# Four layers' tail taken batch by batch: staggered norms, a shorter mix, other places for the activation tables

## What is computed (the reference, cut)

```
x = x + tanh(g_xattn[i]) * xattn_i(layernorm(x), ctx)
x = x + tanh(g_ffn[i])   * ffn_i(layernorm(x))

layer 0: 16-head attention; then six local-attention blocks with feed-forwards
layer 1: a = attend(x -> ctx); c = attend(ctx -> x)
         gate = sigmoid([a, c] @ Wg.T + bg);  result = gate * a + (1 - gate) * c
         ffn: entmax1.5 router over 16 experts (sort, sums, a square root), then gelu
layer 2: attention, then layernorm(result + residual) * gamma + beta
         ffn: top-2 of 8 experts plus a shared one, silu
layer 3: 16-head attention, then top-2 of 8 linear experts
```

## Time and profile before

| | us |
|---|---|
| median of 3 runs | 1364.03 (1363.24 to 1368.13) |
| the profiled execution, its own time | 1366.49 |
| its span in the profile | 1364.5 |
| PE busy | 1259.0 (92%) |
| DVE busy | 973.8 (71%) |
| ACT busy | 933.8 (68%) |

### The profile page before, as it was taken

One profiled execution on the slowest core, in us unless ns is written; L12 is line 12 of the kernel. 1 busy time (PEld: TensorE's weight loads), 2 busy tenths in 40 slices (PEclk: granted clock), 3 DMA queues, 4 the chain that ended last, 5 costly groups with the idle time before them and its releaser, 6 DMA issues. The chain is left out here.

```text
span 1364.5 us, 45293 instructions
## 1 busy us (share of the span) xinstructions
PE 1259.0 (92%) x18140; PEld 906.7 (66%) x18140; DVE 973.8 (71%) x2477; ACT 933.8 (68%) x2301; POOL 744.8 (55%) x753
## 2 busy tenths in 40 slices
PE   6999978999999999999999999999988888999877
PEld 4777635676776777667776776667667767775544
DVE  3666647888888888888888888888843544554766
ACT  5777745677777777777777777777745655643981
POOL 3444437878777877787778877778740042000000
PEclk9999989999999999999999999999999989999998
DMA  4000032222225222522252224222302000000000
GB/s 199 1 2 1 1 109 69 68 63 58 63 61 142 61 63 61 140 60 59 64 143 59 62 62 140 58 61 62 100 9 105 2 1 10 14 0 1 1 1 16
DMA packets 68320, 76.97 MB, mean 56 GB/s; under 512 B 14864, under 2 KB 62992, under 8 KB 67600
## 3 DMA queue, kind: packets, MB, share of 16 engines
q1 hardware_dynamic: 68112, 74.07, 20.4%
HBM read 26.31 MB, written 0.52 MB: 20 GB/s over the span
## 5 line engine op out<-in xcount | busy, mean ns | idle before, releaser
L1073 POOL TENSOR_TENSOR arena<-arena,small 128x512 f32<-128x512 f32 x96 | 100.2, 1044 | 151.1 <-DVE small L956 151.1
L821 ACT ACTIVATE arena<-banks 128x512 f32<-128x512 f32 x96 | 57.4, 598 | 143.8 <-PE banks L653 143.7
L932 DVE TENSOR_TENSOR arena<-banks,rotary 128x512 f32<-128x512 f32 x192 | 131.6, 685 | 31.8 <-ACT arena L791 18.3
L1048 POOL TENSOR_TENSOR arena<-arena 128x512 f32<-128x512 f32 x96 | 122.8, 1279 | 35.9 <-DVE arena L934 35.9
L702 PE MATMUL banks<-arena 64*64 64x32 f32 x6144 | 113.0, 221 | 17.3 <-issue 8.7
L1053 POOL TENSOR_TENSOR arena<-arena 128x512 f32<-128x512 f32 x96 | 122.7, 1279 | 2.2 <-DVE arena L934 2.2
L702 PEld LDWEIGHTS banks<-arena 64*64 64x64 f32 x6144 | 100.7, 135 | 29.4 <-ACT arena L843 12.8
L503 POOL TENSOR_TENSOR arena<-arena,small 128x512 f32<-128x512 f32 x64 | 66.5, 1040 | 86.9 <-DVE small L437 86.9
L616 PE MATMUL banks<-slot,z 128*128 128x512 f32 x192 | 100.9, 607 | 6.9 <-DVE z L1022 3.4
L717 PE MATMUL banks<-arena,slot 128*128 128x128 f32 x768 | 104.0, 278 | 0.5 <-ACT arena L851 0.3
L1060 POOL TENSOR_TENSOR arena<-arena,small 128x512 f32<-128x512 f32 x96 | 100.7, 1049 | 1.2 <-ACT small L831 1.2
(11 more groups left out here) (315 smaller groups left out, 3374.9 us busy)
## 6 DMA issues: line engine op xcount, KB each, us to landing
arena<-arena SPq DMA_DIRECT2D x576, 64.0 KB
slot<-in_pack_dram SPq DMA_DIRECT2D x28, 339.5 KB
arena<-arena SPq DMA_DIRECT2D x288, 32.0 KB
slot<-in_pack_dram SPq DMA_DIRECT2D x2, 2713.5 KB
slot<-in_pack_dram SPq DMA_DIRECT2D x1, 3525.5 KB
slot<-in_pack_dram SPq DMA_DIRECT2D x1, 2316.5 KB
slot<-in_pack_dram SPq DMA_DIRECT2D x4, 337.0 KB
slot<-in_pack_dram SPq DMA_DIRECT2D x7, 158.0 KB
```

The lines of the kernel that those rows point to most:

```text
L932: e.tensor_tensor(rot, made, cos, ALU.mult)
L1048: e.tensor_tensor(m.rot_q[u % ROTS], m.rot_q[u % ROTS], m.sin_q[u % 2], ALU.add).then_inc(s["q_added"], 1)
L1073: e.tensor_tensor(p, p, stretch(m.local_small[u % 4][:, 16:24], SPAN), ALU.subtract).then_inc(s["lowered"], 1)
```

## The change

Seven edits, none of which touches layer 0 or a DMA. New helpers come first. The diff is cut to its core.

```diff
+def pe_ln_staggered(e, s, m, first, ready, idle):
+    for step in range(B + 1):
+        if step < B:
+            e.wait_ge(ready, step + 1)
+            pe_ln_centre(e, s, m, m.bank[2 * step], m.x[step])
+        if step:
+            pe_ln_var(e, s, m, first + step - 1, ln_views(m.ln_tail[step - 1]), m.bank[2 * (step - 1)])
+        pe_idle(e, m, 1, idle)
...
+def act_ln_staggered(e, s, m, first, eps):
+    for step in range(B + 1):
+        if step < B:
+            act_ln_one_square(e, s, m, first, step)
+        if step:
+            act_ln_one_rstd(e, s, m, first, step - 1, eps)
```

The squares of batch b+1 stand ahead of the Ln and Exp of batch b. All six norms take this order. The mix:

```diff
@@ act_tail, mix
+        if k:
+            e.preload_act_table_set("exp_and_others")
         for b in range(B):
             e.wait_ge(s["at_o_made"], 4 * k + b + 1)
@@ dve_tail, mix
     for b in range(B):
         diff = m.t_w[b][:, N:2 * N]
...
+        e.scalar_tensor_tensor(out=m.x[b], in0=m.t_v[b][:, N:2 * N], scalar=m.gates[:, 1:2], in1=m.x[b], ...
+    for b in range(B):
...
+        e.wait_ge(s["mix_tanh"], b + 1)
+        e.scalar_tensor_tensor(out=diff, in0=gate, scalar=1.0, in1=diff, op0=ALU.add, op1=ALU.mult)...
+        e.scalar_tensor_tensor(out=m.x[b], in0=diff, scalar=half_gate, in1=m.x[b], op0=ALU.mult, ...
@@ pe_tail
-    pe_idle(e, m, 1, 16)
...
     pe_idle(e, m, 1, 4)
+    pe_ln_staggered(e, s, m, LN_L1F, s["l1x_done"], 1)
```

```diff
-    e.wait_ge(s["m1_delta"], 1)
-    e.activation(root, delta, ACT.Ln, bias=m.floor).then_inc(s["m1_root"], 1)
...
+    for i, b in enumerate(TURN3):
+        if i == 2:
+            e.wait_ge(s["m1_delta"], 1)
...
+            e.preload_act_table_set("gelu_and_others")
```

The attention of layer 2 issues the scores of batch b-1 right behind the query of batch b, and ACT keeps queries between the norm's steps (L1222 in the new kernel). The residual norm and LN_L2F become one run of eight batches, with one `pe_idle` a step; gamma and beta are multiplied by the gate once, the beta part is added to x ahead of the attention's results, and each batch of x is finished behind its own norm:

```diff
+    for b in range(B):
+        done = e.tensor_scalar(m.x[b], m.x[b], beta, None, ALU.add)
...
+    for b in range(B):
+        dve_ln_out(e, s, LN_RES + b, ln_views(m.ln_tail[b]), m.bank[2 * b], found)
+        e.wait_ge(s["ln_out"], LN_RES + b + 1)
+        e.wait_ge(s["dve_link"], affine)
+        e.scalar_tensor_tensor(out=m.x[b], in0=found, scalar=m.router_stat[3][:, 0:1], in1=m.x[b], ...
```

More of the change, by code:

```diff
@@ L1144, in pe_attention @@
 def pe_attention(e, s, m, k):
[L1145 to L1163, removed]
+    late = 1 if k == 2 else B
+    for step in range(B + late):
+        if step < B:
+            b = step
+            src_q, src_kv, wq, wk, wv = attention_sources(m, k, b)
+            if k == 0:
+                e.wait_ge(s["ln_out"], LN_L1X + b + 1)
+            if k == 1:
+                e.wait_ge(s["found_kept"], b + 1)
+            if k == 2:
+                e.wait_ge(s["ln_out"], LN_L2X + b + 1)
+                e.matmul(m.bank[2 * b][:, 0:N], m.W(7, "W" + wq), src_q, start=True, stop=True,
+                         skip_group_check=True).then_inc(s["p_made"], 1)
+            else:
+                pe_project(e, s, m, k, b, *(m.W(7, "W" + n) for n in (wq, wk, wv)), src_q, src_kv)
+        if step >= late:
+            b = step - late
+            qT, kT = m.t_kT[b][:, 0:N], m.t_kT[b][:, N:2 * N]
+            e.wait_ge(s["p_kept_act"], (16 if k == 2 else 4 * k) + b + 1)
+            for t in range(NT):
+                made = e.matmul(m.bank[2 * b][:, t * N:(t + 1) * N], qT[:, t * P:(t + 1) * P], kT, start=True, stop=True,
+                                skip_group_check=True)
+            made.then_inc(s["at_scored"], 1)
     for b in range(B):
@@ L1350, in pe_tail @@
     e.wait_ge(s["slot0_loaded"], loaded(8))
-    for b in range(B):
+    for b in TURN3:
         b0 = m.bank[2 * b]
@@ L1400, in pe_tail @@
                      skip_group_check=True).then_inc(s["m1_out"], 1)
[L1402 to L1406, removed]
-    pe_attention(e, s, m, 2)
[L1408 to L1419, removed]
+    pe_ln_staggered(e, s, m, LN_L2X, s["l1f_done"], 0)
+    pe_attention(e, s, m, 2)
+    for step in range(2 * B + 1):
+        b = step % B
+        if step < B:
+            e.wait_ge(s["res_done"], b + 1)
+            pe_ln_centre(e, s, m, m.bank[2 * b], m.t_v[b][:, 0:N])
+        elif step < 2 * B:
+            e.wait_ge(s["l2x_done"], b + 1)
+            pe_ln_centre(e, s, m, m.bank[2 * b], m.x[b])
+        if step:
+            first = LN_RES if step <= B else LN_L2F
+            b = (step - 1) % B
+            pe_ln_var(e, s, m, first + b, ln_views(m.ln_tail[b]), m.bank[2 * b])
+        pe_idle(e, m, 1, 1)
     e.wait_ge(s["slot0_loaded"], loaded(8))
@@ L1468, in pe_tail @@
                          start=True, stop=True, skip_group_check=True).then_inc(s["m2_rows"], 1)
[L1470 to L1479, removed]
+    for step in range(B + 3):
+        if step < B:
+            b = step
+            e.wait_ge(s["l2f_done"], b + 1)
+            pe_ln_centre(e, s, m, m.bank[2 * b], m.x[b])
+        if 1 <= step <= B:
+            b = step - 1
+            pe_ln_var(e, s, m, LN_L3X + b, ln_views(m.ln_tail[b]), m.bank[2 * b])
+        if step == 3:
+            e.wait_ge(s["slot1_loaded"], loaded(9))
+        if step >= 3:
+            b = step - 3
+            e.wait_ge(s["ln_out"], LN_L3X + b + 1)
+            e.matmul(m.bank[2 * b][:, 0:N], m.W(9, "Wq"), m.xn[b], start=True, stop=True,
+                     skip_group_check=True).then_inc(s["p_made"], 1)
     for n in range(UNITS3 + LAG3):
@@ L1514, in pe_tail @@
                  skip_group_check=True).then_inc(s["s3_y"], 1)
[L1516 to L1520, removed]
+    pe_ln_staggered(e, s, m, LN_L3F, s["l3x_done"], 0)
     for b in range(B):
@@ L1575, in act_tail @@
     e.preload_act_table_set("natural_log_exp_and_others")
-    act_ln4(e, s, m, LN_L1F, m.ln_tail, m.eps)
+    act_ln_one_square(e, s, m, LN_L1F, 0)
+    for b in range(1, B + 1):
+        if b < B:
+            act_ln_one_square(e, s, m, LN_L1F, b)
+        act_ln_one_rstd(e, s, m, LN_L1F, b - 1, m.eps)
     factor, delta, root = m.router_stat[2], m.router[6], m.router[7]
@@ L1659, in act_tail @@
     act_found3(e, s, m, B - 1)
-    act_ln4(e, s, m, LN_L3F, m.ln_tail, m.eps)
+    act_ln_staggered(e, s, m, LN_L3F, m.eps)
     e.wait_ge(s["m3_lowered"], 1)
```

121 lines of the change are left out of this document (64 added, 57 removed).

## The result

Over 20 executions each, the kernel before took 1365.66 us (median; 1362.76 to 1369.38) and the changed one 1358.09 us (1353.32 to 1368.55). The ratio is 0.9961, with a 95% interval from 0.9948 to 0.9975: faster, by 0.39%, which is within the 0.5% that the prediction called the limit of what can be told. Forecast were 1356.0 us and a range of 1352.5 to 1360.5. One execution of the kernel before, among those timed beside the first experiments, took 1479.33 us at a granted clock of 0.82 and is left out of every comparison.

A forecast was written before the change was run, and what follows sets the result against it. The prediction took the tail's norms as latency-bound through PE, ACT and DVE, layer 3 as bound by ACT's exponentials. Terms summed to 8.0 us off 1366.49, giving 1358.5, less 2.5 for the runs' median: 1356.0, range 1352.5 to 1360.5.

The forecast's parts named there:

- mix and LN_L1F: Mix through its norm: batch-by-batch VectorE steps end the router at 1095.82 instead of 1099.03; gain 3.2 us, bounds 2.9 and 3.4.
- entmax root: Copies and gelu load moved into ACT's idle time at the root; PE's transposes then set the pace; gain 0.1 us.
- LN_L2X, attention 2: Norm and attention start: fourth Ln 0.8 later, batch 3's scores 0.1 earlier; gain 0.1 us, bounds -0.5 and +0.9.
- residual norm, LN_L2F: Two norms merged into one eight-batch run, 10.08 us instead of 13.86; gain 3.7 us, bounds 2.9 and 3.9.
- LN_L3X and the units: Layer 3: new norm order gains 0.1 us; sixteen idle matmuls instead of eight delay the fourth unit, losing 0.3.
- LN_L3F: Last norm: first square at 1328.1 instead of 1329.22, right after the projections; gain 1.1 us, bounds 0.7 and 1.4.
- caution of 0.1 for PE: Merged norms: PE's 1.09 us a batch is just under ACT's 1.11, so gain taken as 3.7, not 3.8.
- with the full clock 0.5: Entmax root: the gain would be 0.5 us instead of 0.1 if PE's transposes ran at full clock.
- staggering by itself gives nothing: LN_L1F: staggered norm needs 5.64 us against 5.60 in the old order, since entmax wants all four batches.
- The drain of the table load: Rival: loads ahead of waiting work cost 1.4 us more at mix and root, giving 1358.7; chance 0.06.
- The round trip: Rival: square-to-Ln trip exceeds ACT's 1.39 us of other work, losing 21 us over 24 steps, 1377.4; chance 0.03.
- The clock rivals: Tail: new half-clock stretches, about 1.5 us each, 1359.0 with two, chance 0.17; or less slow clock, 1353.5, chance 0.08.

The follow-up runs named there:

- the kernel with the residual norm alone: Kernel before plus only the merged eight-batch run of residual norm and LN_L2F, gamma and beta folded into the gate; ratio to before 0.9975.
- the two kernels with fillers: Idle matmuls added in PE's tail waits: to the changed kernel, ratio to before 0.9906; to the kernel before, without those in LN_L3F, 1.0008.
- the late and the early load: Changed kernel with the tanh table loaded behind the bias additions, against its load ahead of them; one execution, mark to first square still 8.69 us.
- all fillers, with or without the new LN_L3X: Changed kernel plus idle matmuls in PE's tail waits, ratio to before 0.9906; also with LN_L3X and third unit as before, 0.9913.
- the root's fillers alone: Changed kernel plus only 14 idle matmuls in PE's wait for the entmax root; ratio to before 0.9925.
- the last kernel: Changed kernel plus idle matmuls in PE's tail waits, with LN_L3X, the third unit and LN_L1F in the order of before; ratio to before 0.9925.
- unwoven: Changed kernel with LN_L2X, LN_L3X and the start of attention 2 put back into the order of before; ratio to before 0.9942.
- the changed kernel with the root undone: Changed kernel with all four kept copies and gelu table load behind the entmax root again; one execution, root's Ln to copy 4.60 us against 4.03.
- the mix alone: Kernel before plus only early tanh table, mix batch by batch and staggered LN_L1F; ratio to before 0.9970.

## Why the prediction held, and where it was off

The time came out 2.1 us above the forecast and inside the range. By class I had put 0.62 on faster by over 0.5%. It is 0.55% by the medians but 0.39% by the ratio, so the class that I gave 0.35, no change that can be told, is what the ratio shows. The gain was 7.6 us by the medians (1365.66 - 1358.09) and 5.3 (3.4 to 7.1) by the ratio; the forecast 8.0 lies outside that interval. The forecast time also rested on three executions, with a median of 1364.03 where 20 gave 1365.66.

Term by term, by the marks at like clock:

| term | forecast | measured |
|---|---|---|
| mix and LN_L1F | 3.2 | 3.17 |
| entmax root | 0.1 | 0.57 (0.15 at half clock) |
| LN_L2X, attention 2 | 0.1 | 0.0 |
| residual norm, LN_L2F | 3.7 | 3.83 |
| LN_L3X and the units | 0.1 - 0.3 | -0.65 |
| LN_L3F | 1.1 | 1.2 at the full clock |
| sum | 8.0 | 8.1 |

That the sum fits so well is partly luck: the root is 0.47 above its term and LN_L3X with the units 0.45 below. In the two large terms the mechanism was right as well as the size; the residual norm needed no caution of 0.1 for PE. In attention 2 the fourth Ln did come later (9.47 us behind the table load against 8.61 in the kernel with the residual norm alone), and the earlier scores made up for it: the last maximum stands at 14.25 and 14.21. LN_L3F is 10.21 - 9.00 = 1.2 between the two kernels with fillers; with the half clock over the projections the profiles give 0.8 to 1.3.

Two steps failed. At the root I took the transposes at the half clock, as in the profile of before, and my own "with the full clock 0.5" was the case. At LN_L3X I had noted that the last products come up to 0.4 later at the full clock and then took the half clock's value. It costs 0.36 at the full clock and 0.0 at half. The idle matmuls cost 0.2 of the 0.3 forecast; the last 0.1 of the -0.65 is no more than the scatter of the units.

A mechanism inside the mix was told rightly (the early table frees the first tanh, not the last), but "staggering by itself gives nothing" was off by 0.36 in LN_L1F: the old order, too, would have run faster once x came early, 5.33 against 5.64, and I compared with its old 5.60.

The rivals. The drain of the table load is not there: 0.00 between the late and the early load, and the square 0.01 behind the load's end. The Trainium skill (ScalarE: Activation LUTs, What ACT_TABLE_LOAD costs) has the 1.38; the trace does not agree, at any of these loads. The round trip never got above ACT's other work: the Ln of the merged norms stand 1.08 to 1.10 apart, the last one 0.89. The clock rivals both happened at once: slow stretches went and one came.

Why the timing shows less than the 8.1, above all by the ratio, is not settled. Twelve of the changed kernel's 20 executions had a granted clock of 0.982 or more and took 1356.8 us in the mean; eight had less and took 1364.4. Of 24 executions of the kernel before, timed beside the first experiments, 19 had such a clock and took 1364.7, and five took 1369.2. That is a gain of 7.9 among the executions with the higher clock and 4.9 among those with the lower one. So a part of what is missing is that more executions fell to the lower clock, 8 of 20 against 5 of 24, and a part lies within that group. Whether the change causes that (by the idle matmuls that it takes out) or the draw does isn't settled: of kernels with nearly its tail, none of 6 (all fillers, with or without the new LN_L3X), 2 of 6 (the root's fillers alone, and the last kernel) and 4 of 8 (unwoven) were below 0.982.

## What to carry to other kernels

In a part bound by latency, whole-batch steps between two norms are the dear ones: here they were worth 3.2 and 3.8 us, while staggering a single norm gave -0.4 to +0.3. Price each term at both clocks that the profiles show, for nobody knows ahead at which it will run: both mis-sized terms came from taking the clock of one profile. And measure a stage between its own marks in several profiles, with the clock of the stretch beside it, since the untouched part in front moved more than the whole change was worth.

## What was not expected

The untouched part: its last copy of turned weights came 10.4 us apart in two executions of code that is the same up to there. The first row is the changed kernel with the root undone, the second the mix alone.

```profile
1078.24 0.60 ACT L1238 ACTIVATE arena<-banks 128x512 f32<-128x512 f32 x1 [0.20 <-PE banks L1202]
```
```profile
1088.68 0.60 ACT L1230 ACTIVATE arena<-banks 128x512 f32<-128x512 f32 x1 [0.20 <-PE banks L1195]
```

Ahead of this mark the clock was at half for 20.5 us in the first profile and for 41.0 in the second. That is a part of it and not all: in the kernel before it was 20.5 too, and the mark stood at 1081.48.

The slow stretches fell at other places in nearly every profile. They can also cost nothing. In the kernel without the weaves one lay over the experts of layer 3 (1334 to 1337), in before another (1344 to 1347), and from the end of the last router matmul to the end of the span it took 29.1 us in both, as in the kernel with fillers, which had none there. In the changed kernel one began at 1331.2, over that matmul, and the same way took 30.5.
